# A mixture-of-experts stage on one core: the down product in three passes, combine weights through DMA and GpSimd

## The chip, the cores and the metric

The kernel runs on one core of a Trainium2 chip. The metric is the device time of one execution in microseconds. A core has five engines that run side by side and meet at semaphores: TensorE (PE; its weight loads are PEld), VectorE (DVE), ScalarE (ACT), GpSimd (POOL) and SyncE (SP), which here issues DMA transfers. TensorE has two clock levels, 1.2 and 2.4 GHz; the granted clock in the profile is the share of the higher one.

## The reference, cut to what matters

The network has four layers on 4608 tokens of 128 channels (8 images of 24 by 24). The change is in the second, a mixture of eight experts and one shared expert, all 64 wide:

```
x_flat = layernorm(t)                                  # (4608, 128)
shared = silu(x_flat @ shared_gate) * (x_flat @ shared_up) @ shared_down
probs  = softmax(x_flat @ router)                      # (4608, 8)
combine[n, e] = probs[n, e] if e is one of the two largest of row n else 0
gate = silu(x_flat @ W_gate[e]);  up = x_flat @ W_up[e]
y    = (gate * up) @ W_down[e]
t    = t + shared + sum over e of combine[:, e] * y[e]
```

Every token goes through all eight experts; the combine weight, mostly zero, is multiplied into the hidden row ahead of the down product.

## The kernel before, in words

The program is a chain of blocks; a block ends when all engines are through with their part of it. Three of them matter here.

*The router* (lines 615 to 702) normalises and transposes the tokens. It keeps them twice in SBUF with channels on the partitions: `xTH`, rounded to the F32R format that TensorE takes in one pass, and `xTL`, the rounded-off rest.

*The weights block* (lines 704 to 741) finds the top two for the second half of the tokens (the first half was done earlier), and transposes all combine weights, in nine lots of 512 tokens, from tokens on partitions to experts on partitions. ScalarE writes each lot's rounded values into `cT` (L723) and VectorE the rests (L715).

*The expert block* (lines 767 to 960) goes over 12 chunks of 384 tokens. A chunk has five units: four pairs of experts (`k` 0 to 3, 128 hidden rows: two experts of 64) and the shared expert (`k` 4). Unit `u` counts through all 60. For a pair TensorE makes

- the gate product in three passes, high by high, high by low, low by high (`product3`, L807, L808, L811), into PSUM bank `q = u % 2`,
- the combine weights spread over the 64 rows of each expert, a product of `cT` with a matrix of ones (`sel`, L826), into bank 4,
- the up product in three passes into bank `2 + q`,
- the down product (L838), in full precision, from the hidden rows `h4`; the five units of a chunk add up in bank 5 or 6.

ScalarE takes the SiLU of the gate bank (`s4`, L879). VectorE multiplies bank 4 by it (`t4`, L918), and that by the up bank (`h4`, L923, in SBUF). For the shared expert gate and up lie in the two halves of one bank and VectorE multiplies once (L927). When a chunk is done, ScalarE copies its bank (`y4`, L892), TensorE transposes it in three pieces into bank 7 (L849, `back`) and VectorE adds it to the residual `R` (L907).

The order on each engine is written out by hand: TensorE issues `feed(u + 1)` and then `down(u)`; ScalarE runs one unit ahead. The first and last two chunks are straight code, the ten between them a hardware loop (`Fori`) over two chunks.

In the last two chunks VectorE also does the next layer's first statistics, one step `ahead(a)` for each of the last ten units: for `a` 0 to 5 three `bn_stats` (L941), with seven small instructions of `norm_moments` after every third; for `a` 6 to 8 three normalisations (L948). Between them GpSimd takes a power (`norm_rstd`, L158), and `ahead(6)` waits for the first one (`rs5`). Otherwise GpSimd only clears buffers at the start of this block (L770, L781), and SP writes zeros into the DRAM tensor `slots`, seven transfers of 768 KB (L792, L796).

Of the kernel before, what the change touches and what calls it, by code (L numbers as in the profile page):

```python
# [25 lines left out]
F32 = mybir.dt.float32  # L26
# [56 lines left out]
def metaformer_kernel(nc, A, out):  # L83
    ctx = ExitStack()
    with ctx:
# [40 lines left out]
        slots = nc.dram_tensor("slots", [2 * SLOTS + N, C], F32, kind="Internal").ap()  # L126

# [50 lines left out]
        sel = sb("sel", [P, E2 // 2 * P], F32R)  # L178
# [217 lines left out]
        with nc.Block() as block:  # L396
# [163 lines left out]
        dve3b, ex3, spl3, cps3, cH3, cL3, cz3, sl3, wz3 = (  # L560
            sem(n) for n in "dve3b ex3 spl3 cps3 cH3 cL3 cz3 sl3 wz3".split())
        cT = lsb("cT", [P, N], F32R)
# [51 lines left out]

        with nc.Block() as block:
            @block.gpsimd
            def _(pool):
                nc.gpsimd.memset(wd[H2:P, NB2 - 1, :], 0.0).then_inc(wz3, 1)
                pool.wait_ge(wz3, 1)
                nc.gpsimd.memset(cT[:].bitcast(F32), 0.0).then_inc(cz3, 1)  # L620
# [43 lines left out]
            def _(act):  # L664
# [11 lines left out]
                nc.scalar.activation(sel[:], konst[:, K_SEL:K_SEL + E2 * H2], ACT.Copy)  # L676
# [27 lines left out]
        with nc.Block() as block:  # L704
            @block.vector
            def _(dve):
# [5 lines left out]
                for b in range(NT // TB):  # L712
                    dve.wait_ge(cH3, b + 1)
                    at = slice(b * TB * P, (b + 1) * TB * P)
                    nc.vector.tensor_tensor(cT[32:32 + E2, at], bank[b % 8][:E2, :], cT[0:E2, at].bitcast(F32),  # L715
                                            ALU.subtract).then_inc(cL3, 1)

            @block.scalar
            def _(act):
                def high_weights(first, end):  # L720
                    for b in range(first, end):
                        act.wait_ge(cps3, b + 1)
                        nc.scalar.activation(cT[0:E2, b * TB * P:(b + 1) * TB * P], bank[b % 8][:E2, :],  # L723
                                             ACT.Copy).then_inc(cH3, 1)

                act.wait_ge(cz3, 1)
                high_weights(0, EARLY)
                act.wait_ge(sl3, 2)
                nc.scalar.activation(ex8[1], d8[1], ACT.Exp).then_inc(ex3, 1)
                high_weights(EARLY, NT // TB)  # L730

            @block.tensor
            def _(pe):
                for b in range(NT // TB):
                    if b == EARLY:
                        pe.wait_ge(spl3, 2)
                    if b >= 8:
                        pe.wait_ge(cL3, b - 7)
# [5 lines left out]
        s4 = [lsb(f"s4_{q}", [P, CH]) for q in range(2)]  # L744
        t4 = [lsb(f"t4_{q}", [P, CH]) for q in range(2)]
        h4 = [lsb(f"h4_{q}", [P, CH]) for q in range(2)]
        y4 = [lsb(f"y4_{p}", [P, CH]) for p in range(2)]
        g_ps, u_ps, s_ok, h_ok, dn, yS, zt = (sems(n) for n in "g_ps u_ps s_ok h_ok dn yS zt".split())
        cb_ps, t_ok, R_ok = sem("cb_ps"), sem("t_ok"), sem("R_ok")
# [3 lines left out]
        TRIPS = N // CH // 2  # L753
        UB = 2 * NB2
        UPT = 2 * (NB2 - 1)
# [1271 lines left out]
```

## Time and profile before

| | |
|---|---|
| median of 3 runs | 450.92 us (449.1 to 452.47) |
| the profiled execution | 448.98 us |
| its span, first to last instruction | 446.8 us |
| granted TensorE clock, mean | 0.865 |
| TensorE busy | 373.4 us, 84% of the span |
| VectorE, ScalarE, GpSimd busy | 305.2, 154.1, 127.8 us |

Busy time is the time in which an engine has an instruction in work. The ends of matrix products are modelled in the profile and neighbouring products overlap, so the distance from the start of one to the start of the next is what a product costs. Lines of the timeline give start, duration, engine and source line; "x3" behind a line means that three alike were merged; "q" behind an engine's name is its queue, and the bracket at the end is the idle time ahead of the instruction and what ended it. Times are microseconds from the start of the span.

### The profile page before, as it was taken

How to read it: one execution, taken by the hardware profiler on the slowest of the kernel's cores; microseconds unless marked ns; L12 is line 12 of the kernel's file. 1: busy time of each engine (PE TensorE's matmuls, PEld its weight loads, DVE VectorE, ACT ScalarE, POOL GpSimd, SP SyncE). 2: the span in 40 equal slices, each digit the busy share in tenths (PEclk: the TensorE clock that was granted, in tenths of full speed). 3: DMA queues.
4: the chain of work that ended last, by engine and by line, in shares of the span. 5: the costliest groups of instructions: out<-in, count | busy, mean ns of one | idle time of the engine just before them, and what ended most of it. 6: DMA issues, size and time to landing. Idle time of an engine off the chain costs nothing. (4 is left out here: it accounts for less than half of the span.)

```text
span 446.8 us, 6657 instructions
## 1 busy us (share of the span) xinstructions
PE 373.4 (84%) x2125; PEld 315.9 (71%) x2125; DVE 305.2 (68%) x949; ACT 154.1 (34%) x324; POOL 127.8 (29%) x141
## 2 busy tenths in 40 slices
PE   5955949968999999998756999999789796699880
PEld 5955949947888887887445899999779762693330
DVE  5846884885555566569656576876574969259997
ACT  2221154434333333332214455475465530240000
POOL 5750143006500000002000366010116567005773
PEclk9999555558999999999856599999999976699996
DMA  8930510005700000000011011111001011772335
GB/s 182 278 119 12 164 43 1 1 0 203 292 1 0 0 1 0 0 0 0 2 28 43 10 35 35 34 35 35 1 1 55 13 41 48 256 264 82 95 99 147
DMA packets 22890, 29.66 MB, mean 66 GB/s; under 512 B 4104, under 2 KB 18249, under 8 KB 22606
## 3 DMA queue, kind: packets, MB, share of 16 engines
q1 hardware_dynamic: 18350, 22.47, 17.1%
q0 software_dynamic: 1728, 3.54, 2.6%
q10 hardware_dynamic: 2784, 3.29, 2.1%
q8 instruction: 15, 0.25, 0.2%
q14 instruction: 13, 0.11, 0.1%
HBM read 13.48 MB, written 12.78 MB: 59 GB/s over the span
## 5 line engine op out<-in xcount | busy, mean ns | idle before, releaser
L158 POOL TENSOR_TENSOR rstd<-sm,neg_half 128x9 f32<-128x9 f32 x10 | 18.0, 1804 | 203.3 <-DVE sm L152 203.3
L807 PE MATMUL ps<-wide,gu_w 128*128 (+1 forms) x108 | 51.9, 481 | 2.2 <-PEq L704 2.2
L879 ACT ACTIVATE s<-ps 128x384 f32<-128x384 f32 (+1 forms) x60 | 29.5, 492 | 67.4 <-PE ps L811 67.0
L1767 PE MATMUL ps<-V,wide 128*128 128x129 f32 x400 | 51.3, 276 | 0.0
L838 PE MATMUL ps<-h,wd 128*128 128x384 f32 x120 | 49.8, 497 | 1.6 <-DVE h L923 1.2
L1767 PEld LDWEIGHTS ps<-V,wide 128*128 128x128 f32 x400 | 48.4, 192 | 0.1
L918 DVE TENSOR_TENSOR t<-ps,s 128x384 f32<-128x384 f32 x48 | 26.8, 557 | 30.3 <-ACT s L879 30.0
L1811 PE MATMUL ps<-ew,xTd 128*128 128x512 f32 x72 | 38.2, 669 | 3.6 <-DVE R L1480 3.5
L1480 DVE SCALAR_TENSOR_TENSOR R<-ps,dense_w,R 128x128 f32<-128x128 f32 x144 | 38.3, 343 | 1.3 <-PE ps L1811 1.1
L1232 DVE TENSOR_REDUCE mx<-ps 128x1 f32<-128x576 f32 (+1 forms) x40 | 29.8, 749 | 12.8 <-PE ps L1735 12.7
L811 PE MATMUL ps<-wide,gu_w 128*128 (+1 forms) x108 | 37.0, 343 | 0.3 <-DVE t L918 0.3
L808 PE MATMUL ps<-wide,gu_w 128*128 (+1 forms) x108 | 37.0, 342 | 0.0
L1578 ACT ACTIVATE wide<-ps 128x576 f32<-128x576 f32 (+1 forms) x40 | 25.9, 649 | 30.1 <-PE ps L1747 30.0
L1142 POOL DMA_INDIRECT slots<-xn,sidx x27 | 26.4, 976 | 26.0 <-DVE sidx L1359 18.8
L923 DVE TENSOR_TENSOR h<-ps,t 128x384 f32<-128x384 f32 x48 | 26.8, 558 | 4.3 <-DVE t L918 3.1
L1735 PE MATMUL ps<-Q,K 97*128 97x288 f32 x80 | 22.5, 372 | 7.4 <-DVE mx L1232 4.6
L1811 PEld LDWEIGHTS ps<-ew,xTd 128*128 128x128 f32 x72 | 14.2, 212 | 19.9 <-issue 11.7
L1173 POOL DMA_INDIRECT xn<-slots,gidx x18 | 18.6, 1035 | 31.6 <-DMA slots<-wide 26.4
L807 PEld LDWEIGHTS ps<-wide,gu_w 128*128 128x128 f32 x108 | 20.8, 193 | 8.7 <-issue 2.4
L808 PEld LDWEIGHTS ps<-wide,gu_w 128*128 128x128 f32 x108 | 20.9, 194 | 6.2
L838 PEld LDWEIGHTS ps<-h,wd 128*128 128x128 f32 x120 | 21.0, 188 | 5.7 <-DVE h L923 4.6
L811 PEld LDWEIGHTS ps<-wide,gu_w 128*128 128x128 f32 x108 | 20.7, 191 | 0.7 <-DVE t L918 0.7
(252 smaller groups left out, 810.8 us busy)
## 6 DMA issues: line engine op xcount, KB each, us to landing
slots<-zrow SPq DMA_DIRECT2D x7, 768.0 KB, 7.7
xe<-slots SPq DMA_DIRECT2D x16, 192.0 KB, 4.0
slots<-wide ACTq DMA_DIRECT2D x16, 192.0 KB, 2.9
xall<-in_x SPq DMA_DIRECT2D x8, 288.0 KB, 6.1
out<-R SPq DMA_DIRECT2D x9, 192.0 KB, 2.1
Q<-sQK SPq DMA_DIRECT2D x8, 144.0 KB, 2.4
K<-sQK SPq DMA_DIRECT2D x8, 144.0 KB, 2.5
ew<-in_ew SPq DMA_DIRECT2D x1, 1024.0 KB, 5.4
```

Source lines behind the costliest of these rows:

```text
L807: nc.tensor.matmul(o, gu_w[0][:, w], xTH[:, at], start=True, stop=False)
L808: nc.tensor.matmul(o, gu_w[0][:, w], xTL[:, at], start=False, stop=False)
L811: return nc.tensor.matmul(o, gu_w[1][:, w], xTH[:, at], start=False, stop=True)
L838: nc.tensor.matmul(bank[5 + p][:, :CH], wd[:, k, :], h4[q][:], start=k == 0, stop=k == NB2 - 1).then_inc(dn[q], 1)
L879: nc.scalar.activation(s4[q][:r], bank[q][:r, :CH], ACT.Silu).then_inc(s_ok[q], 1)
L918: d.did(nc.vector.tensor_tensor(t4[q][:], bank[4][:, :CH], s4[q][:], ALU.mult))
L923: nc.vector.tensor_tensor(h4[q][:], bank[2 + q][:, :CH], t4[q][:], ALU.mult).then_inc(h_ok[q], 1)
L1142: nc.gpsimd.indirect_dma_start(slots, bass.IndirectOffsetOnAxis(sidx[g % 2][:, t:t + 1], 0), xn_buffer(g)[:, t, :], None).then_inc(sc6[g % ...
L1232: nc.vector.tensor_reduce(mx[n % 2][:m, k:k + 1], halves(psum[e_pair(n, k)], m), AX.XY, ALU.max).then_inc(mx_ok, 1)
L1480: nc.vector.scalar_tensor_tensor(at, of, weight, at, ALU.mult, ALU.add).then_inc(s9, 1)
L1767: last = nc.tensor.matmul(bank[6 + k // 3][:, k % 3 * (C + 1):(k % 3 + 1) * (C + 1)], PT[n % 2][:, jk, i0:i0 + P], V[n % 2][:, jk, :], sta ...
L1811: last = nc.tensor.matmul(bank[b], xTd[:, (t - DENSE0) * P:(t - DENSE0 + 1) * P], ew[:, 4 * quad:4 * quad + 4, :].rearrange("c e f -> c (e ...
```

## The change

The combine weights are no longer split or multiplied out on TensorE. ScalarE copies them as they are; SP stores them to a DRAM tensor `combine_w` in two parts and loads them back, spread over the 64 rows of each expert, one chunk at a time into two buffers `cB` (`spread`, two DMAs of 393 KB each). The first two chunks are spread in the weights block, later ones when GpSimd has done all multiplies of two chunks before. GpSimd multiplies `cB` by the SiLU (`t4`); VectorE multiplies the up bank by `t4` in place, so that the hidden product stays in PSUM (three up banks, 2 to 4, in turn; the shared unit's product stays in its gate bank). ScalarE copies it rounded into `hH`, VectorE subtracts that from it into `hL`, and the down product is made in three F32R passes from `hH`, `hL` and a split weight `wdH`, `wdL`. The down product runs three units behind the feed (`LAG`). The loop is written out. GpSimd's buffer clears come one by one behind the multiplies of chunks 2 to 8, its two powers after the last multiply; SP's zero fills go between the spreads.

```diff
-        sel = sb("sel", [P, E2 // 2 * P], F32R)
+        wdH, wdL = (sb(n, [P, NB2, C], F32R) for n in ("wdH", "wdL"))
+        cB = [pt_tiles[0][:, 0:E2 // 2, 0:CH], pt_tiles[1][:, 0:E2 // 2, P:P + CH]]
+        def spread(sp, c):
+            at = slice(CH * c, CH * (c + 1))
+            by_half = combine_w[:, at].rearrange("(k two) n -> two k n", two=2)
+            for half in range(2):
+                sp.dma_start(cB[c % 2][H2 * half:H2 * (half + 1)],
+                             by_half[half:half + 1].to_broadcast([H2, E2 // 2, CH])).then_inc(cin[c % 2], 16)
...
-                for b in range(NT // TB):
-                    dve.wait_ge(cH3, b + 1)
-                    at = slice(b * TB * P, (b + 1) * TB * P)
-                    nc.vector.tensor_tensor(cT[32:32 + E2, at], bank[b % 8][:E2, :], cT[0:E2, at].bitcast(F32),
-                                            ALU.subtract).then_inc(cL3, 1)
+            @block.sync
+            def _(sp):
+                for j, (first, end) in enumerate(((0, EARLY), (EARLY, NT // TB))):
+                    at = slice(first * TB * P, end * TB * P)
+                    sp.wait_ge(cH3, end)
+                    sp.dma_start(combine_w[:, at], cT[:, at]).then_inc(cs[j], 16)
+                    if j == 0:
+                        sp.wait_ge(cs[0], 16)
+                        for c in range(2):
+                            spread(sp, c)
+                sp.wait_ge(cs[1], 16)
...
+                act.wait_ge(wz3, 1)
+                nc.scalar.activation(wdH[:], wd[:], ACT.Copy).then_inc(wdh, 1)
                 high_weights(EARLY, NT // TB)
...
+        CHUNKS = N // CH
+        UNITS = CHUNKS * NB2
+        LAG = 3
+        def shared(u):
+            return u % NB2 == NB2 - 1
+        def pair(u):
+            return (NB2 - 1) * (u // NB2) + u % NB2
+        def pair_unit(v):
+            return v // (NB2 - 1) * NB2 + v % (NB2 - 1)
+        def held(u):
+            return bank[u % 2][0:H2, :CH] if shared(u) else bank[2 + pair(u) % 3][:, :CH]
...
             @block.gpsimd
-                for ap, value in firsts:
-                    z.did(nc.gpsimd.memset(ap.bitcast(F32), value))
-                    z.wait()
+                for u in range(UNITS):
+                    if shared(u):
+                        continue
+                    v, c = pair(u), u // NB2
+                    pool.wait_ge(cin[c % 2], 32 * (c // 2 + 1))
+                    pool.wait_ge(s_ok, u + 1)
+                    if v >= 2:
+                        pool.wait_ge(h_ok, pair_unit(v - 2) + 1)
+                    nc.gpsimd.tensor_tensor(t4[v % 2][:], cB[c % 2][:, u % NB2, :], s4[u % 2], ALU.mult).then_inc(t_ok, 1)
+                    if v == 8:
+                        nc.gpsimd.memset(zrow[:], 0.0).then_inc(z4, 1)
+                    elif v > 8 and v - 9 < len(firsts):
+                        ap, value = firsts[v - 9]
+                        pool.wait_ge(t_ok, v + 1)
+                        z.did(nc.gpsimd.memset(ap.bitcast(F32), value))
+                        z.wait()
+                z.wait()
                 for g in range(BEFORE):
                     pool.wait_ge(var5, g + 1)
                     norm_rstd(GT, g, P, rs5)
             @block.sync
+                for c in range(2, 4):
+                    sp.wait_ge(t_ok, (NB2 - 1) * (c - 1))
+                    spread(sp, c)
                 sp.wait_ge(z4, 1)
+                for c in range(4, CHUNKS):
+                    sp.wait_ge(t_ok, (NB2 - 1) * (c - 1))
+                    spread(sp, c)
+                    for k in range(4 * (c - 4), min(4 * (c - 3), SLOTS // (SR * 12))):
+                        sp.dma_start(slots[k * SR * 12:(k + 1) * SR * 12, :].rearrange("(p t) c -> p t c", t=12),
+                                     zrow[:SR]).then_inc(zf4, 16)
+                    if c - 8 in range(NT // 12):
...
             @block.tensor
+                def feed(u):
+                    c, k = divmod(u, NB2)
+                    tokens = slice(CH * c, CH * (c + 1))
+                    if u >= 2:
+                        pe.wait_ge(s_ok, u - 1)
+                        if shared(u - 2):
+                            pe.wait_ge(hl_ok, u - 1)
+                    product3(bank[u % 2][:, :CH], slice(2 * k * P, (2 * k + 1) * P), tokens).then_inc(g_ps, 1)
+                    if not shared(u):
+                        v = pair(u)
+                        if v >= 3:
+                            pe.wait_ge(hl_ok, pair_unit(v - 3) + 1)
+                        product3(bank[2 + v % 3][:, :CH], slice((2 * k + 1) * P, (2 * k + 2) * P), tokens).then_inc(u_ps, 1)
+                def down(u):
...
+                    pe.wait_ge(hh_ok, u + 1)
+                    nc.tensor.matmul(o, wdH[:, k, :], hH[q][:], start=k == 0, stop=False)
+                    nc.tensor.matmul(o, wdL[:, k, :], hH[q][:], start=False, stop=False)
+                    pe.wait_ge(hl_ok, u + 1)
+                    nc.tensor.matmul(o, wdH[:, k, :], hL[q][:], start=False, stop=k == NB2 - 1).then_inc(dn, 1)
...
+                for u in range(UNITS + LAG):
+                    if u < UNITS:
+                        feed(u)
+                    if u >= LAG:
+                        down(u - LAG)
+                    c, k = divmod(u - LAG - 1, NB2)
+                    if k == 0 and c >= 1:
+                        back(c - 1)
+                back(CHUNKS - 1)
             @block.scalar
+                silu(0)
+                for u in range(UNITS + LAG + 1):
+                    if u + 1 < UNITS:
+                        silu(u + 1)
+                    if u < UNITS:
+                        high(u)
+                    c, k = divmod(u - LAG + 1, NB2)
+                    if k == 0 and c >= 1:
+                        channels(c - 1)
             @block.vector
+                def hidden(u):
+                    if shared(u):
+                        dve.wait_ge(s_ok, u + 1)
+                        nc.vector.tensor_tensor(held(u), bank[u % 2][H2:P, :CH], s4[u % 2][:H2], ALU.mult).then_inc(h_ok, 1)
+                    else:
+                        dve.wait_ge(u_ps, pair(u) + 1)
+                        dve.wait_ge(t_ok, pair(u) + 1)
+                        nc.vector.tensor_tensor(held(u), held(u), t4[pair(u) % 2][:], ALU.mult).then_inc(h_ok, 1)
+                def low(u):
+                    dve.wait_ge(hh_ok, u + 1)
+                    r = rows(u)
+                    nc.vector.tensor_tensor(hL[u % 3][:r], held(u), hH[u % 3][:r].bitcast(F32), ALU.subtract).then_inc(hl_ok, 1)
...
+                for u in range(UNITS + LAG + 2):
+                    if u < UNITS:
+                        hidden(u)
+                    if 1 <= u <= UNITS:
+                        low(u - 1)
+                    c, k = divmod(u - LAG - 2, NB2)
+                    if k == 0 and c >= 1:
+                        residual(c - 1)
+                    if UNITS - 2 * NB2 <= u < UNITS:
+                        if u == UNITS - 2 * NB2:
+                            dve.wait_ge(R_ok, CHUNKS // 2)
+                        ahead(u - UNITS + 2 * NB2)
+                residual(CHUNKS - 1)
```

## Rows read from the trace of the kernel before

**Rows 1.** Windows: stretch, length, busy time by engine, granted clock, DMA share, GB/s.
```profile
122.30:131.50 9.20, 9.20 (x46) 7.55 (x44) 5.45 (x11) 2.95 (x6) 0.00 (x0) 1.00 0.00 1
```

**Rows 2.** Timeline of a pair unit inside the loop: start, duration, engine, line.
```profile
125.34 0.34 PE L811 MATMUL ps<-wide,gu_w 128*128 x1
...
125.71 0.49 ACT L879 ACTIVATE s<-ps 128x384 f32<-128x384 f32 x1
...
126.05 0.34 PE L811 MATMUL ps<-wide,gu_w 128*128 x1
...
126.22 0.81 PE L838 MATMUL ps<-h,wd 128*128 128x384 f32 x2
...
127.92 0.34 PE L811 MATMUL ps<-wide,gu_w 128*128 x1
```

**Rows 3.** Timeline of the weights block and the start of the expert block.
```profile
96.27 0.59 ACT L723 ACTIVATE cT<-ps 8x512 fp32r<-8x512 f32 x1 [0.27 <-PE ps L740]
...
98.23 5.46 DVE L715 TENSOR_TENSOR cT<-ps,cT 8x512 fp32r<-8x512 f32 x9
...
101.02 1.63 ACT L723 ACTIVATE cT<-ps 8x512 fp32r<-8x512 f32 x3 [0.27 <-PE ps L740]
...
104.17 0.41 PE L807 MATMUL ps<-wide,gu_w 128*128 128x384 f32 x1 [2.18 <-PEq L704]
...
113.67 0.63 PE L807 MATMUL ps<-wide,gu_w 128*128 128x384 f32 x1
```

**Rows 4.** Timeline where chunk 11 begins and TensorE waits for VectorE.
```profile
205.97 0.56 DVE L923 TENSOR_TENSOR h<-ps,t 128x384 f32<-128x384 f32 x1
206.45 0.67 DVE L941 BATCH_NORM_STATS2 st<-R 128x6 f32<-128x128 f32 x3
...
206.58 0.91 PE L838 MATMUL ps<-h,wd 128*128 128x384 f32 x2 [0.96 <-DVE h L923]
...
207.04 0.64 PE L807 MATMUL ps<-wide,gu_w 128*128 128x384 f32 x1
...
207.51 0.33 PE L808 MATMUL ps<-wide,gu_w 128*128 128x384 f32 x1
```

**Rows 5.** Timeline of the end of the expert block.
```profile
212.37 0.85 DVE L948 TENSOR_SCALAR xn<-R,sm,rstd 128x128 f32<-128x128 f32 x3
...
217.98 0.91 PE L838 MATMUL ps<-h,wd 128*128 128x384 f32 x2 [0.45 <-DVE h L927]
...
220.06 0.56 DVE L907 TENSOR_TENSOR R<-R,ps 128x384 f32<-128x384 f32 x1 [2.13 <-PE ps L849]
```

**Rows 6.** Groups by line, GpSimd: count, busy us, mean ns of one, idle before.
```profile
L158 POOL TENSOR_TENSOR rstd<-sm,neg_half 128x9 f32<-128x9 f32 x10 | 18.0, 1804 | 203.3 <-DVE sm L152 203.3
...
L253 POOL TENSOR_TENSOR kvq<-scaled,bkvq 96x288 f32<-96x288 f32 x8 | 6.2, 791 | 2.6 <-DVE scaled L296 2.6
...
L781 POOL MEMSET Q<- 1x640 f32 x6 | 3.8, 627 | 0.3
...
L487 POOL TENSOR_TENSOR nmr<-sm,rstd 128x9 f32<-128x9 f32 x2 | 0.4, 208 | 0.2
```

**Rows 7.** DMA issues on the page: count, KB each, median us to landing.
```profile
K<-sQK SPq DMA_DIRECT2D x8, 144.0 KB, 2.5
```

**Rows 8.** Windows, in the midst of the zero fills; the last number is GB/s.
```profile
107.00:108.00 1.00, 1.00 (x5) 1.00 (x4) 0.13 (x2) 0.49 (x1) 0.93 (x2) 0.53 1.05 424
```

**Rows 9.** Timelines of GpSimd and VectorE in the first block.
```profile
13.99 1.54 POOL L253 TENSOR_TENSOR kvq<-scaled,bkvq 96x288 f32<-96x288 f32 x2
...
15.04 0.53 DVE L280 TENSOR_TENSOR sm<-st 96x12 f32<-96x12 f32 x1
15.49 0.17 DVE L281 TENSOR_TENSOR sm<-st 96x12 f32<-96x12 f32 x1
```

**Rows 10.** Windows in the stage behind: busy time by engine, then the granted clock.
```profile
225.00:230.00 5.00, 1.31 (x5) 0.59 (x4) 2.17 (x6) 1.23 (x2) 0.00 (x0) 0.50 0.26 59
315.00:320.00 5.00, 2.75 (x22) 2.31 (x21) 2.20 (x10) 3.01 (x8) 2.00 (x2) 1.00 0.00 0
```

More of the change, by code:

```diff
@@ L741, in _ @@
                     last.then_inc(cps3, 1)
-        s4 = [lsb(f"s4_{q}", [P, CH]) for q in range(2)]
+        s4 = [wstage[:, q * CH:(q + 1) * CH] for q in range(2)]
         t4 = [lsb(f"t4_{q}", [P, CH]) for q in range(2)]
[L746 to L749, printed above, removed]
+        hH = [lsb(f"hH{q}", [P, CH], F32R) for q in range(3)]
+        hL = [lsb(f"hL{q}", [P, CH], F32R) for q in range(3)]
+        y4 = [xTf[p][:] for p in range(2)]
+        g_ps, u_ps, s_ok, t_ok, h_ok, hh_ok, hl_ok, dn, yS, zt, R_ok, wdl = (
+            sem(n) for n in "g_ps u_ps s_ok t_ok h_ok hh_ok hl_ok dn yS zt R_ok wdl".split())
         zrow = lsb("zrow", [P, 12, C])
@@ L852, in trip @@
-                def trip(i, first, final):
-                    for u in range(UB):
-                        if u + 1 < UB:
-                            feed(i, u + 1)
-                        elif not final:
-                            feed(i + 1, 0)
-                        down(i, u)
-                        if u == 1 and not first:
-                            back(i - 1, 1)
-                        if u == NB2 + 1:
-                            back(i, 0)
-                pe.wait_ge(wz3, 1)
@@ new lines, in back @@
+                def back(c):
+                    pe.wait_ge(yS, c + 1)
+                    if c:
+                        pe.wait_ge(R_ok, c)
+                    for t in range(3):
+                        last = nc.tensor.transpose(bank[7][:, t * P:(t + 1) * P], y4[c % 2][:, t * P:(t + 1) * P], ident)
+                    last.then_inc(zt, 1)
+                pe.wait_ge(wz3, 1)
+                for u in range(UNITS + LAG):
[6 more added lines that the diff above has]
+                        back(c - 1)
@@ L894, in _, with silu @@
-                silu(0, 0)
-                trip(0, False)
-                with act.Fori(1, TRIPS - 1) as i:
-                    trip(i, False)
-                trip(TRIPS - 1, True)
+                def silu(u):
+                    act.wait_ge(g_ps, u + 1)
+                    if u >= 2:
+                        if shared(u - 2):
+                            act.wait_ge(h_ok, u - 1)
+                        else:
+                            act.wait_ge(t_ok, pair(u - 2) + 1)
+                    r = rows(u)
+                    nc.scalar.activation(s4[u % 2][:r], bank[u % 2][:r, :CH], ACT.Silu).then_inc(s_ok, 1)
@@ new lines, in high, with channels @@
+                def high(u):
+                    act.wait_ge(h_ok, u + 1)
+                    if u >= 3:
+                        act.wait_ge(dn, u - 2)
+                    nc.scalar.activation(hH[u % 3][:rows(u)], held(u), ACT.Copy).then_inc(hh_ok, 1)
+                def channels(c):
+                    act.wait_ge(dn, NB2 * (c + 1))
+                    if c >= 2:
+                        act.wait_ge(zt, c - 1)
+                    nc.scalar.activation(y4[c % 2], bank[5 + c % 2][:, :CH], ACT.Copy).then_inc(yS, 1)
```

147 lines of the change are left out of this document (27 added, 120 removed).

## The prediction

> **What bounds the kernel now.** I read the busy time of each engine in one stretch of the stage first, then the order of time inside one unit, then the two ends of the stage, and last the rows that price the new work. In the stretch from 122.3 to 131.5 us, about one chunk of 384 tokens, TensorE is busy all of 9.20 us at full clock, VectorE 5.45, ScalarE 2.95 and GpSimd nothing [rows 1]. So TensorE sets the pace and three engines have room. Inside a unit the single passes (F32R) follow each other every 0.175 us: the last pass of a gate product starts at 125.34 and that of the up product at 126.05, four passes later. The last pass of the next up product starts at 127.92, so a pair unit takes 1.87 us [rows 2]. It holds seven such passes, 1.225 us; what is left, 0.645 us, is the full-precision down product. The chunks agree: chunk 1 begins at 113.67 and chunk 11 at 207.04, ten chunks of 9.34 us [rows 3, 4]. The stage runs from 104.17 to 220.06 + 0.56 = 220.62 us [rows 3, 5].
>
> **What is removed from TensorE.** Each of 48 pair units loses the selection product (0.175), and each of 60 down products goes from 0.645 to three passes, 0.525. A pair unit becomes 9 × 0.175 = 1.575 us. The shared unit becomes 6 × 0.175 = 1.05, and with it come the three transposes of the output, 0.34. A chunk would be 4 × 1.575 + 1.05 + 0.34 = 7.69 us, 1.65 under now, if TensorE could still run without waiting. That is the whole of the possible gain, some 18 us.
>
> **The path that is put in its place.** The hidden products now stay in PSUM, and a bank is free only when the low half has been taken from it. For pairs there are three banks; for gate products two, and the shared unit's product lies in its gate bank. So the gate product of the second pair after a shared unit s, unit s + 2, waits for low(s). VectorE's order is hidden(u), then low(u − 1): low(s) stands behind hidden(s + 1), and that waits for ScalarE and GpSimd on unit s + 1. Counted from the start of gate(s + 1): its last pass starts at 0.35; ScalarE starts 0.37 later and takes 0.49 [rows 2], 1.21. GpSimd's multiply is not in the trace at 384 columns. The nearest rows are 0.791 for 288 columns and 0.208 for 9, so 0.99 for 384 [rows 6]. Releases between engines cost 0.03 to 0.08; I take 0.05, so hidden(s + 1) starts at 2.30. Two VectorE instructions without a wait between them start 0.48 apart and take 0.56, and TensorE starts 0.05 after VectorE's end [rows 4]: 2.30 + 0.48 + 0.56 + 0.05 = 3.39. A restart costs 0.11 more (0.93 from L838 to the L808 that follows in [rows 4], against 0.645 + 0.175 where it runs on). So gate(s + 2) starts 3.50 us after gate(s + 1), where TensorE has work for 1.575. TensorE stands still for 1.9 us in each chunk, and a chunk is 3.50 + 3 × 1.575 + 1.05 + 0.34 = 9.61 us, not 7.69. Against 9.34 that is 0.27 more. Queued behind this wait on TensorE are all later feeds and the down products of the last two units.
>
> In the other units the same loop has room: up(u + 3) waits for low(u), which ends at 1.575 + 3.39 = 4.97, and TensorE gets there at 3 × 1.575 + 0.525 = 5.25. ScalarE's second copy (another 0.49) and the second VectorE pass stay below 1.575 a unit.
>
> The in-place write of hidden into PSUM has no row. Between 0 more and one more pass over 384 columns (0.4 us, from 0.48 a pass) I take 0, since every VectorE row here with one PSUM operand costs the same 0.56; the 0.4 would be paid in each chunk, 4 to 5 us.
>
> **Ends of the stage, and what moves.** *Start.* Before, the block with the weights ends with VectorE's low halves at 98.23 + 5.46 = 103.69 and the first product comes at 104.17 [rows 3]. These halves go; SP takes their place. The first store of weights can go at 96.86, the second after the last ScalarE copy at 102.65. A store of 144 KB took 2.5 us to landing [rows 7], which gives 105.15. But between them SP queues two spreads of 0.79 MB, 3.7 us at the 424 GB/s of [rows 8], which begin about 100.3 and end near 104. The block ends between 104.7 and 106.7; I take 105.5, so +1.8. *Chunk 0* took 9.50; it loses four selections and four down products and has only two of the new ones, since these run three units behind: −0.70 − 2.58 + 1.05 = −2.2, of which the wait for the first low half gives back about 0.6: −1.6. *Ten chunks*: 10 × 0.27 = +2.7. *Memsets*: 27 of them, the common one 0.63 [rows 6], now stand between the multiplies. GpSimd's 0.99 + 0.63 + two waits exceeds 1.575, so it slips up to 0.4 within a chunk and catches up while TensorE waits; +0.3 over three chunks. *Spreads*: a chunk's DMA may start when the multiplies of two chunks before are done, some 11 us ahead, and 0.79 MB take 2 us; even behind four zero fills of 0.77 MB it lands in 13 of some 21. Nothing, unless the queue holds it 8 us longer. The last zero fill is issued over two chunks before the end: 0. The wdH copy and the wdL difference lie under waits: 0. Loop unrolling: its price now is inside the 1.87; 0.
>
> *End.* This is the largest term. The last two chunks carry the next stage's statistics on VectorE, and ahead(6), in unit 56, waits for the first power on GpSimd. Before, GpSimd was idle there. Now both powers (1.80 each [rows 6]) stand behind the last multiply, that of unit 58. From the first gate product of chunk 11: VectorE comes about 1.3 late, as the seven moments instructions (0.17 each [rows 9]) find no room in chunk 10; hidden(55) starts at 2.30 + 1.3 = 3.6, gate(56) at 3.6 + 0.48 + 0.56 + 0.05 + 0.11 = 4.8, gate(58) two units later at 7.95, its multiply ends 1.26 + 0.99 later at 10.2, and the power at 12.05. Only then do three ahead steps (0.77 each, from three in 0.85 [rows 5]) and four passes of 0.48 run to hidden(59) at 16.3; then 0.56, copy 0.49, low 0.56 and three releases: 18.05. Before, the last down product took 0.91 and the end came 2.64 after its start [rows 5]; with a last pass of 0.34 it is 2.07: 20.1. Before it was 220.62 − 207.04 = 13.6. So +6.5.
>
> Sum: 1.8 − 1.6 + 2.7 + 0.3 + 6.5 = +9.7 us. The profiled execution took 448.98 us (span 446.8 and 2.2 around it), 1.9 under the median of the runs and just under the lowest. 448.98 + 9.7 = 458.7; from the median it is 460.6. I forecast 460.
>
> **GpSimd and VectorE at once.** One row shows them in each other's way: a VectorE sum of two SBUF operands took 0.53 where the next takes 0.17, and it ended with the GpSimd operation that ran from 13.99 to 15.53 [rows 9]. Hidden and low read one operand each from PSUM, and no row shows such an instruction beside a multiply. The Trainium skill ("SBUF — State Buffer", Who interferes with whom) says that only two SBUF inputs or a two-port mode collide with GpSimd's reads. By that rule only the moments suffer, up to 1 us at the end, and the sum stays; the trace agrees as far as it goes. Without it, low would wait out each multiply: the third rival.
>
> **The rivals.** *Faster: TensorE keeps its pace.* Had low(s) its turn before hidden(s + 1), the loop would close with 7.69 a chunk: 10 × 1.92 less than forecast, 441 us. For it: TensorE is the bound now and loses 18 us of work. Against it: the written order, and no idle engine can reorder it. Faster than before begins where the 3.50 falls under 3.2, and by over 1% near 2.2, before the multiply could end. 7%. *Same:* multiply 0.8 (the 288-column price), shorter releases and a part of the end hidden: −0.35 × 11 − 3 = 453 us. 18%. *Slower still:* PSUM write at 0.4 more, or VectorE held off by each multiply, 0.8 a pair unit in three of a chunk: 2.4 × 11 = 26, to 486; the PSUM write alone 465. 12% together. *Clock:* full clock held in a stretch with TensorE busy 2.75 of 5 us; it stood at half with 1.31 of 5 busy [rows 10]. The new stage has 7.69 of 9.61 us. If half were granted, a chunk's products would take 15.4: 60 us more, 520. 3%. The Trainium skill ("TensorE: Matmul & The Clock Gate", HAM oscillation — how this bites in real kernels) warns that waits between bursts of matmuls bring the slow clock back; the first row of the two bears it out, the second shows a share of work well under this stage's at full clock.
>
> **How the numbers follow.** Forecast 60%: 460. Its own bounds: multiply 0.8 to 1.2 gives −2 to +5; the start −0.8 to +1.2; the PSUM write up to +5. With the case of no change the range is 452 to 470; beyond lie 7 + 8 + 3 in 100. What a measurement of this kernel can tell from no change is about 1%, 446.4 to 455.4 us: faster 0.07, same 0.20, slower 0.73.
>
> **What would show it.** In the changed profile: one TensorE gap of near 1.9 us in each chunk, ended by VectorE's low subtraction; chunks 9.6 apart; multiplies of 0.99; first product near 106; VectorE idle for about 4 us in the last chunk until GpSimd's power. A chunk spacing under 9 would break the first step, a multiply far from 1.0 its size, an end under 16 us after chunk 11's start the last.

## The result and the profile after

The changed kernel takes 474.06 us (median of 472.82 to 475.29) against 450.52 for the kernel before: a ratio of 1.049, 95% interval 1.0445 to 1.0541. That is slower by 23.5 us, above the range of the prediction (452 to 470). The profiled execution has a span of 473.5 us, 26.7 more than before; the two profiled executions (448.98 and 475.29 us) stand 2.8 us further apart than the medians. The tables by stage go by these two.

The stage by chunk: chunk 0 starts with the first pass of a gate product (L850) at 109.66, chunk 1 at 117.92, chunk 11 at 219.27, and the last residual sum (L954) ends at 243.43. The chunks from 0 to 10 take 8.26, 9.71, 10.19, 10.16, 10.16, 10.08, 9.95, 11.41, 10.04, 9.87 and 9.78 us; before, the mean of chunks 1 to 10 was 9.34 [rows 3, 4]. So:

| part of the span | before | after | difference | forecast |
|---|---|---|---|---|
| up to the first product | 104.17 | 109.66 | +5.5 | +1.8 |
| chunk 0 | 9.50 | 8.26 | -1.2 | -1.6 |
| chunks 1 to 10 | 93.37 | 101.35 | +8.0 | +3.0 (2.7 + 0.3) |
| chunk 11 to the end of the stage | 13.58 | 24.16 | +10.6 | +6.5 |
| all stages behind | 226.18 | 230.07 | +3.9 | 0 |
| sum | 446.8 | 473.5 | +26.7 | +9.7 |

The windows of the ten chunks in the middle (length, busy time by engine, granted clock, DMA share, GB/s) answer to [rows 1]:

```profile
117.92:219.27 101.35, 81.52 (x452) 76.60 (x451) 57.72 (x121) 50.11 (x111) 53.44 (x68) 0.98 0.47 133
```

TensorE, which before stood still in these ten chunks only for the 0.96 us of [rows 4], now does so for 19.8 of 101.35 us, 2.0 a chunk. The timeline of chunk 10 shows where. It starts with gate(s + 1) and ends with gate(s + 2):

```profile
209.49 0.42 PE L850 MATMUL ps<-wide,gu_w 128*128 128x384 f32 x1
...
210.15 0.57 DVE L940 TENSOR_TENSOR ps<-ps,wstage 64x384 f32<-64x384 f32 x1
...
210.30 0.49 ACT L911 ACTIVATE wstage<-ps 128x384 f32<-128x384 f32 x1
...
210.75 0.48 ACT L917 ACTIVATE hH<-ps 64x384 fp32r<-64x384 f32 x1
...
210.92 1.00 POOL L814 TENSOR_TENSOR t<-wide,wstage 128x384 f32<-128x384 f32 x1 [1.93 <-ACT wstage L911]
...
212.02 0.57 DVE L944 TENSOR_TENSOR ps<-ps,t 128x384 f32<-128x384 f32 x1 [0.72 <-POOL t L814]
212.50 0.54 DVE L949 TENSOR_TENSOR hL<-ps,hH 64x384 fp32r<-64x384 f32 x1
...
213.18 0.42 PE L850 MATMUL ps<-wide,gu_w 128*128 128x384 f32 x1 [1.87 <-DVE hL L949]
```

Hidden(s), the product of the shared unit, is there at 210.72 and its high half at 211.23, but low(s) waits until 212.50 behind hidden(s + 1), which waits for the multiply. TensorE's wait of 1.87 ends with low(s), the row with 64 partitions.

The start, in the timeline of the block of the weights, and the spreads in the view of the DMA issues:

```profile
99.11 2.49 ACT L740 ACTIVATE cT<-ps 8x512 f32<-8x512 f32 x5 [1.21 <-PE ps L758]
99.52 2.64 SPq L624 DMA_DIRECT2D wide<-combine_w  x4
102.20 0.50 SPq L728 DMA_DIRECT2D combine_w<-cT  x1
...
109.66 0.66 PE L850 MATMUL ps<-wide,gu_w 128*128 128x384 f32 x1 [8.84 <-PEq L713]
```
```profile
DMA packets 1104, 1.66 MB, mean 162 GB/s; under 512 B 72, under 2 KB 1096, under 8 KB 1096
...
wide<-combine_w SPq DMA_DIRECT2D x4, 384.0 KB, 6.2
```

All arithmetic of the block is over at 101.60. SyncE issues the second store at 102.20, behind four spreads of 384 KB, and the block waits for it until 109.6. In the second fence, from 99.5 to 109.7 us, 1.66 MB move at a mean of 162 GB/s; the traffic fills 29 of that view's 40 slices, which gives some 220 GB/s while it lasts (estimate: 162 × 40 / 29), not the 424 of [rows 8]. TensorE idles for 8.84 us and starts chunk 0 at half clock (passes 0.32 apart).

The end, in the timeline from chunk 11 on:

```profile
219.27 0.42 PE L850 MATMUL ps<-wide,gu_w 128*128 128x384 f32 x1
...
224.31 0.66 PE L850 MATMUL ps<-wide,gu_w 128*128 128x384 f32 x1 [2.91 <-DVE hL L949]
...
230.04 0.34 PE L850 MATMUL ps<-wide,gu_w 128*128 128x384 f32 x1
...
231.39 1.01 POOL L814 TENSOR_TENSOR t<-wide,wstage 128x384 f32<-128x384 f32 x1 [0.94 <-issue]
```
```profile
232.36 3.56 POOL L159 TENSOR_TENSOR rstd<-sm,neg_half 128x9 f32<-128x9 f32 x2
234.20 0.86 DVE L969 TENSOR_SCALAR xn<-R,sm,rstd 128x128 f32<-128x128 f32 x3 [5.81 <-POOL rstd L159]
...
242.87 0.56 DVE L954 TENSOR_TENSOR R<-R,ps 128x384 f32<-128x384 f32 x1 [2.25 <-PE ps L887]
```

VectorE waits 5.81 us for the power behind the last multiply. The clock in the windows (the third number from the end; 1.00 is 2.4 GHz, 0.50 is 1.2):

```profile
182.00:184.00 2.00, 2.00 (x7) 2.00 (x8) 0.26 (x1) 0.82 (x2) 0.10 (x1) 0.51 1.07 329
222.00:224.00 2.00, 0.00 (x0) 0.00 (x0) 1.97 (x7) 0.48 (x1) 0.48 (x1) 0.75 0.01 4
224.00:230.00 6.00, 5.70 (x18) 5.73 (x19) 3.17 (x14) 1.74 (x4) 1.56 (x2) 0.51 0.00 0
264.00:274.00 10.00, 7.66 (x33) 6.96 (x33) 5.28 (x14) 3.76 (x6) 0.00 (x0) 0.50 0.13 30
```

Half clock was granted for 3.4 us in chunk 7 (11.41 us where its neighbours take 9.95 and 10.04), and again from 223.0, within the wait that ends at 224.31, until 229.8. The last row lies 20.6 to 30.6 us behind the stage's end; the same stretch of the kernel before had 0.67, for about 3 us of full clock in it:

```profile
241.00:251.00 10.00, 7.43 (x36) 6.68 (x36) 5.52 (x15) 3.94 (x7) 0.00 (x0) 0.67 0.13 30
...
331.80 0.69 DVE L1232 TENSOR_REDUCE mx<-ps 64x1 f32<-64x576 f32 x1
```

The last of these VectorE maxima, 111.18 us behind the stage's end before, comes 114.21 behind it after (357.64 - 243.43): 3.0 of the 3.9 us are lost by there, in the same 702 matrix products.

```profile
357.64 0.69 DVE L1261 TENSOR_REDUCE mx<-ps 64x1 f32<-64x576 f32 x1
```

### The profile page after: what moved, and what is told of

It is laid out like the page before. It is cut to its first block and busy times, and to the rows that moved or that the text cites. A ratio compares the mean times of both kernels' runs of the same rounds, so it can differ in the third digit from the quotient of the medians.

```text
span 473.5 us, 6654 instructions
## 1 busy us (share of the span) xinstructions
PE 366.4 (77%) x2137; PEld 323.5 (68%) x2137; DVE 302.6 (64%) x953; ACT 178.5 (38%) x384; POOL 171.0 (36%) x188
## 5 line engine op out<-in xcount | busy, mean ns | idle before, releaser
L814 POOL TENSOR_TENSOR t<-wide,wstage 128x384 f32<-128x384 f32 x48 | 48.4, 1009 | 101.5 <-ACT wstage L911 89.9
L850 PE MATMUL ps<-wide,gu_w 128*128 128x384 f32 x108 | 41.0, 379 | 31.9 <-DVE hL L949 22.9
L944 DVE TENSOR_TENSOR ps<-ps,t 128x384 f32<-128x384 f32 x48 | 27.2, 566 | 48.3 <-POOL t L814 45.8
L1796 PE MATMUL ps<-V,wide 128*128 128x129 f32 x400 | 53.3, 283 | 0.0
L1796 PEld LDWEIGHTS ps<-V,wide 128*128 128x128 f32 x400 | 50.3, 198 | 0.1
L911 ACT ACTIVATE wstage<-ps 128x384 f32<-128x384 f32 (+1 forms) x60 | 29.3, 489 | 48.0 <-PE ps L852 47.5
L850 PEld LDWEIGHTS ps<-wide,gu_w 128*128 128x128 f32 x108 | 21.8, 202 | 36.6 <-issue 34.9
L851 PE MATMUL ps<-wide,gu_w 128*128 128x384 f32 x108 | 38.5, 356 | 0.0
L852 PE MATMUL ps<-wide,gu_w 128*128 128x384 f32 x108 | 38.3, 354 | 0.0
L917 ACT ACTIVATE hH<-ps 128x384 fp32r<-128x384 f32 (+1 forms) x60 | 29.4, 489 | 21.2 <-DVE ps L944 18.4
L949 DVE TENSOR_TENSOR hL<-ps,hH 128x384 fp32r<-128x384 f32 (+1 forms) x60 | 32.8, 548 | 0.4
L879 PE MATMUL ps<-hL,wdH 128*128 128x384 f32 x60 | 21.6, 360 | 4.1 <-DVE hL L949 4.0
L851 PEld LDWEIGHTS ps<-wide,gu_w 128*128 128x128 f32 x108 | 22.0, 204 | 0.0
```

The lines of the kernel that those rows point to most:

```text
L814: nc.gpsimd.tensor_tensor(t4[v % 2][:], cB[c % 2][:, u % NB2, :], s4[u % 2], ALU.mult).then_inc(t_ok, 1)
L850: nc.tensor.matmul(o, gu_w[0][:, w], xTH[:, at], start=True, stop=False)
L851: nc.tensor.matmul(o, gu_w[0][:, w], xTL[:, at], start=False, stop=False)
L852: return nc.tensor.matmul(o, gu_w[1][:, w], xTH[:, at], start=False, stop=True)
L949: nc.vector.tensor_tensor(hL[u % 3][:r], held(u), hH[u % 3][:r].bitcast(F32), ALU.subtract).then_inc(hl_ok, 1)
L1796: last = nc.tensor.matmul(bank[6 + k // 3][:, k % 3 * (C + 1):(k % 3 + 1) * (C + 1)], PT[n % 2][:, jk, i0:i0 + P], V[n % 2][:, jk, :], sta ...
```

## The experiments

Theory A is that of the prediction with these corrections: separate waits, each with its place (start, low(s), memsets, powers), which add up. The rivals stand in each expectation. All edits are to the changed kernel, and are shown cut to the lines that matter. From each trace, one execution a kernel: first product, mean of chunks 1 to 10, chunk 11 to the end of the stage, and the rest of the span.

| run | median us | against before (95%) | first product | chunk | last chunk | rest |
|---|---|---|---|---|---|---|
| kernel before | 450.52 | | 104.17 | 9.34 | 13.58 | 226.2 |
| changed kernel | 474.06 | 1.049 (1.045 to 1.054) | 109.66 | 10.14 | 24.16 | 230.1 |
| e1_wait | 469.68 | 1.041 (1.034 to 1.049) | 103.17 | 10.14 | 24.15 | 230.8 |
| e2_low | 461.11 | 1.019 (1.012 to 1.026) | 109.51 | 8.78 | 22.51 | 232.4 |
| e3_pow | 469.67 | 1.040 (1.034 to 1.047) | 109.54 | 10.27 | 18.55 | 227.6 |
| e4_half | 461.89 | 1.022 (1.014 to 1.030) | 109.18 | 9.43 | 20.80 | 229.1 |
| e5_all | 448.61 | 0.992 (0.989 to 0.996) | 103.23 | 8.78 | 17.88 | 231.4 |
| e6_hold | 439.06 | 0.971 (0.965 to 0.977) | 103.15 | 7.92 | 17.82 | 229.9 |
| e7_early | 437.04 | 0.966 (0.960 to 0.972) | 103.00 | 8.20 | 12.22 | 228.7 |
| e8_memset | 475.08 | 1.049 (1.042 to 1.056) | 109.41 | 10.24 | 24.30 | 230.7 |
| e9_spread | 432.76 | 0.956 (0.951 to 0.961) | 103.86 | 7.79 | 12.48 | 230.5 |
| e10_hold | 449.09 | 0.995 (0.991 to 0.999) | 109.57 | 7.96 | 21.65 | 228.1 |
| e11_f32 | 435.83 | 0.963 (0.956 to 0.970) | 103.48 | 8.27 | 12.15 | 226.3 |

**The second store (e1_wait).**

```diff
             # SyncE, block of the weights
-            sp.wait_ge(cs[1], 16)
             # SyncE, expert block
             for c in range(4, CHUNKS):
                 sp.wait_ge(t_ok, (NB2 - 1) * (c - 1))
+                if c == 5:
+                    sp.wait_ge(cs[1], 16)
```

> The wait of SyncE for the second store of weights is moved from the end of the weights block to just ahead of the first spread that reads what it wrote (that of chunk 5). Theory A (the block with the weights ends late because that store, issued at 102.20, lies on its queue behind four spreads that move 1.57 MB until about 109.5): the first product comes when the last ScalarE copy and the transposes are done, near 102.5 instead of 109.66, but the first multiply still needs chunk 0's spread, about 104.5; the stage begins 6 to 7 us earlier and the whole kernel is 5 to 7 us faster, 467 to 469. Rival B (the spreads themselves hold chunk 0: the multiply waits for the same bytes wherever the wait stands): first product early, but chunk 0 longer by the same 5 to 7 us; no change, 472 to 475.

The timeline has the store at 102.09, behind the spreads as before, and the first product 1.1 us later:

```profile
102.09 0.49 SPq L728 DMA_DIRECT2D combine_w<-cT  x1
...
103.17 0.41 PE L850 MATMUL ps<-wide,gu_w 128*128 128x384 f32 x1 [2.46 <-PEq L713]
```

The first product comes 6.5 us earlier, and chunk 0 takes 8.03: theory A. The span of the trace falls by 5.9 us (the stage ends 6.7 earlier, the rest is 0.7 longer), the median by only 4.4 (expected 5 to 7).

**The low half first (e2_low).**

```diff
+                first = u >= 1 and shared(u - 1)
+                if first:
+                    low(u - 1)
                 if u < UNITS:
                     hidden(u)
-                if 1 <= u <= UNITS:
+                if 1 <= u <= UNITS and not first:
                     low(u - 1)
```

> VectorE takes the low half of a shared unit ahead of the next hidden product. Theory A (TensorE stands still once a chunk because low(s) waits behind hidden(s+1), which waits for ScalarE and GpSimd on unit s+1): low(s) starts when ScalarE's copy of hidden(s) is done, about 1.3 us earlier; the gap of 1.9 to 2.1 us goes below 0.9 and chunks come every 8.7 to 9.0 us instead of 10.1; ten chunks 11 to 14 us, the kernel 460 to 463. Rival B (GpSimd's multiply with its waits and memsets is the pace whatever the order, 4 multiplies and one gap a chunk): the gap moves to another product, chunks stay at 9.8 to 10.2, 471 to 475.

```profile
189.76 1.07 DVE L949 TENSOR_TENSOR hL<-ps,hH 128x384 fp32r<-128x384 f32 x2
...
189.94 0.99 POOL L814 TENSOR_TENSOR t<-wide,wstage 128x384 f32<-128x384 f32 x1 [1.50 <-DVE ps L940]
190.98 0.42 PE L850 MATMUL ps<-wide,gu_w 128*128 128x384 f32 x1 [0.76 <-DVE hL L949]
191.03 0.57 DVE L944 TENSOR_TENSOR ps<-ps,t 128x384 f32<-128x384 f32 x1 [0.20 <-POOL t L814]
```

In the timeline low(s) now runs ahead of hidden(s + 1), in one row with low(s - 1); gate(s + 2) starts while the multiply is just ending, and hidden(s + 1) comes after it. The gap is 0.76 instead of 1.87, the chunk 8.78, and the kernel 13 us faster than the changed one. So the order on VectorE held TensorE, not the pace of GpSimd.

**The first power earlier (e3_pow).**

```diff
                 # GpSimd, behind each multiply
+                if u == UNITS - 7:
+                    pool.wait_ge(var5, 1)
+                    norm_rstd(GT, 0, P, rs5)
...
-            for g in range(BEFORE):
-                pool.wait_ge(var5, g + 1)
-                norm_rstd(GT, g, P, rs5)
+            pool.wait_ge(var5, 2)
+            norm_rstd(GT, 1, P, rs5)
```

> GpSimd takes the first power after the multiply of unit 53 instead of after that of unit 58; the second stays last. Theory A (VectorE's 5.8 us of idle time at 228.4 to 234.2 are the wait for a power that is queued behind the last multiply, and the half clock behind it follows from TensorE's idle time): the 5.8 us go, chunk 11 to the end of the stage takes 16.5 to 19 us instead of 24.2, the kernel 466 to 469. Rival B (the end is paced by the half clock that was granted before the power was due, from 222 to 230): 1 to 3 us, 471 to 473.

The last chunk falls by 5.6 us, from 24.16 to 18.55: the wait of 5.8 was the one for the power. TensorE still idles 2.9 us ahead of gate(56), for low(54) behind the statistics, and gate(56) to gate(58) takes 4.77 us, from 226.8 on at half clock, so rival B has the other part. In this trace chunks 3 and 10 took 11.49 and 11.34, and the median gained 4.4 of the 5 to 8 expected.

**Half a multiply (e4_half).** This kernel leaves out half of each multiply: the other half of `t4` stays zero, so it is a probe and no version to use.

```diff
-nc.gpsimd.tensor_tensor(t4[v % 2][:], cB[c % 2][:, u % NB2, :], s4[u % 2], ALU.mult)
+nc.gpsimd.tensor_tensor(t4[v % 2][:, :CH // 2], cB[c % 2][:, u % NB2, :CH // 2], s4[u % 2][:, :CH // 2], ALU.mult)
```

> Leaves work out: GpSimd multiplies only the first 192 of 384 columns (the other half of its result stays zero), all waits kept. By the slope between 1.01 us at 384 columns and 0.79 at 288 the multiply takes 0.56. Theory A (the multiply lies on the chain from gate(s+1) to gate(s+2), once a chunk): the gap shrinks by 0.45, the chunks with memsets also lose their excess of 0.3; chunks 9.3 to 9.6 instead of 10.1, the kernel 5 to 8 us faster, 466 to 469. Rival B (GpSimd paces every unit): four times 0.45 a chunk, chunks near 8.5, 455 to 458. Rival C (TensorE or VectorE paces): no change.

The multiply takes 0.59, the chunks 9.28 to 9.47: 0.71 less each on average. The chunks without memsets (1, 9 and 10) fall by 0.42, the multiply once a chunk; the rest is memsets that now fit and the spell at half clock in chunk 7, which is gone. Rival B, four times the multiply, would have been 8.5. The kernel gained 12 us, more than expected: chunk 11 and chunk 0 pay for the multiply too (3.4 and 0.4), and none of the ten chunks ran at half clock.

**The three together (e5_all)**: the diffs of e1, e2 and e3.

> The three edits together: the wait for the second store moved to the spread of chunk 5, the low half of a shared unit taken ahead of the next hidden product, the first power after the multiply of unit 53. Theory A (three separate losses, which add): stage from 103.2, chunks 8.8, chunk 11 to the end 17 to 18.5; -6.5 in the start, -13.5 in ten chunks, -6 at the end, of which the next stage gives some back: 449 to 453, as the kernel before. Rival B (the losses overlap, since the clock of TensorE falls wherever it waits): 455 to 460.

They add, to within 4 us: 448.61 is 25.5 under the changed kernel, where the three alone took 4.4, 13.0 and 4.4 off the median. Chunk 0 gives back 1.2 of the start (9.42 us): with the store out of the way, the first multiply waits until 105.80 for its spread, and TensorE stands still for 1.82 us behind it. The kernel is within 1% of the one before the change, though its chunks have 1.65 us less of TensorE's work.

**A bank for the shared product (e6_hold, e10_hold).** The first has the three edits as well, the second nothing else.

```diff
-return bank[u % 2][0:H2, :CH] if shared(u) else ...     # held(u)
+return bank[6][0:H2, :CH] if shared(u) else ...
-pe.wait_ge(hl_ok, u - 1)                                # feed, behind a shared unit
+pe.wait_ge(h_ok, u - 1)
-o, q = bank[5 + c % 2][:, :CH], u % 3                   # down; channels likewise
+o, q = bank[5][:, :CH], u % 3
                     # ScalarE: channels(c - 1) moved ahead of silu(u + 1)
```

> As the three together, and besides the shared unit's product gets a bank of its own (the second bank of the down product, which keeps one; ScalarE then copies a chunk's output ahead of the next silu), so that gate(s+2) waits for hidden(s) alone and no longer for low(s). Theory A (the rest of the gap, 0.9 us a chunk and 1.2 with memsets, is the held gate bank): chunks 7.8 to 8.1, 7 to 9 us less than with the three edits, 441 to 445, faster than the kernel before. Rival B (GpSimd's multiply of 1.0 and its waits and memsets leave no more than 8.7 a chunk): within 2 us of the three edits. Rival C (one bank for the down product makes TensorE wait for ScalarE's copy once a chunk, 0.5 to 1.4 us): 445 to 450.

> The changed kernel with one edit: the shared unit's product has a bank of its own, and the down product one bank. Theory A (the one gap of TensorE a chunk is the held gate bank, nothing else): chunks without memsets 7.7, those with memsets 8.2 to 8.4; 10 chunks 20 us less, start and end as in the changed kernel; 453 to 456, about the kernel before. Rival B (without the low half taken first the wait only moves, to the up product three pairs on, which waits for low(u)): chunks 8.5 to 9, 460 to 464.

With this one edit the chunks with neither memsets nor statistics (1 and 9) take 7.59 and 7.66, the whole of the work that the prediction counted (chunk 10, with statistics, 8.03), and the kernel takes 449.09, within 1% of the kernel before; expected were 453 to 456, but chunk 11 and the rest gained 2.5 and 2.0 as well. In the timeline of e10_hold gate(s + 2) follows gate(s + 1) by 1.65 us while the multiply runs:

```profile
125.43 0.42 PE L850 MATMUL ps<-wide,gu_w 128*128 128x384 f32 x1
...
126.86 1.02 POOL L814 TENSOR_TENSOR t<-wide,wstage 128x384 f32<-128x384 f32 x1 [1.94 <-ACT wstage L911]
...
127.08 0.34 PE L850 MATMUL ps<-wide,gu_w 128*128 128x384 f32 x1
```

So the held gate bank alone was the gap. With the other three edits it gives 439.06.

**Memsets and statistics (e8_memset, e7_early, e9_spread).** The memsets go into the block ahead of the stage, all at once; in e7 also `UNITS - 2 * NB2` becomes `UNITS - 4 * NB2` for the statistics, and the powers follow the multiplies of units 43 and 48. In e9 the statistics are cut up:

```diff
-                if u % 3 == 2:
-                    norm_moments(f, ins, GT, g, P, EPS_C, var5)
+    # stats_of(g): three bn_stats, then the moments in four pieces, "yield" behind each;
+    # next_stage(): both groups, then the nine normalizations one by one
+                if UNITS - 5 * NB2 + 1 <= u < UNITS:
+                    next(ahead, None)
```

> The changed kernel with nothing but the 27 memsets moved into the block ahead of the stage. Theory A (each of the seven chunks with memsets pays 0.3, since GpSimd's multiply, memset and two waits take 1.78 where a unit has 1.575): chunks 2 to 8 fall from 10.1 to 9.8, 2.0 to 2.5 us in all, 471 to 472. Rival B (memsets collide with VectorE where they go): the product of that block later by 1 to 4 us, first product later, 473 to 476.

> As the one before, and besides the 27 memsets moved into the block ahead of the expert stage, where GpSimd has nothing to do, and the statistics of the next stage with both powers two chunks earlier. Theory A (memsets cost 0.3 in each of seven chunks, the statistics and the 2.3 us of normalization lie on VectorE's path in the last chunk): 2 us for the memsets and 3 to 5 at the end, 435 to 440. Rival B (VectorE's sums of two SBUF operands in the block of the weights collide with the memsets): that block grows by 1 to 4 us and eats it up; 440 to 444.

> As the version with early statistics, but these are cut into 23 pieces, one a unit over the last 24 units, and the second power comes a chunk later. Theory A (in that version the ninth and tenth chunk took 11.25 and 8.62 instead of 7.67, because seven statistics instructions at a time stand ahead of a hidden product, one of them held 1.00 us beside a multiply, and because the multiply of the next chunk waited for a power that waited for them): these chunks fall to 7.7 to 8.2, 3 to 4.5 us less, 433 to 434. Rival B (the power itself, 1.80 us, does not fit beside four multiplies in a chunk): 1.5 us of it stay, 435 to 437.

By its time e8 shows nothing (475.08), and rival B is not the reason: the first product comes at 109.41, not later. By its chunks it shows two things that cancel: seven chunks take 9.76 to 9.78, with nothing left of the 0.3 that chunks with memsets paid, and three take 11.33 to 11.35. In each of those three the clock fell for a spell:

```profile
124.00:126.00 2.00, 2.00 (x9) 2.00 (x8) 1.02 (x2) 0.54 (x2) 0.21 (x1) 0.65 0.00 0
155.00:157.00 2.00, 2.00 (x10) 2.00 (x9) 1.02 (x2) 0.62 (x2) 0.21 (x2) 0.72 0.09 17
186.00:188.00 2.00, 2.00 (x11) 2.00 (x10) 1.02 (x2) 0.75 (x2) 0.34 (x2) 0.79 0.21 86
```

A spell at half clock costs 1.57 us (11.34 against 9.77). In e7 the last chunk takes 12.22 instead of 17.82, but the statistics then weigh on their own chunks. Its timeline has one row like that of [rows 9]:

```profile
179.65 1.00 DVE L143 TENSOR_TENSOR sm<-st 128x9 f32<-128x9 f32 x1
180.58 0.16 DVE L144 TENSOR_TENSOR sm<-st 128x9 f32<-128x9 f32 x1
```

The first sum of two SBUF operands ran from 179.65 to 180.65, as long as GpSimd's multiply (179.62 to 180.63), the next 0.16. Hidden and low, with one operand in PSUM, keep 0.57 and 0.55 beside a multiply (low in 32 of 48 pair units of e7). The normalisations, 0.34 each alone, are held as well: in e11 six of nine take 0.71 to 1.16. In pieces (e9) chunks 9 and 10 fall from 11.25 and 8.62 to 8.35 and 7.67, and the kernel is the fastest: 432.76, 4.4% under the kernel before.

**One full-precision down product (e11_f32).** As e9, with the hidden product in SBUF, no high and low halves, and

```diff
-nc.tensor.matmul(o, wdH[:, k, :], hH[q][:], start=k == 0, stop=False)
-nc.tensor.matmul(o, wdL[:, k, :], hH[q][:], start=False, stop=False)
-nc.tensor.matmul(o, wdH[:, k, :], hL[q][:], start=False, stop=k == NB2 - 1).then_inc(dn, 1)
+nc.tensor.matmul(o, wd[:, k, :], h4[q][:], start=k == 0, stop=k == NB2 - 1).then_inc(dn, 1)
```

> The down product of the version with cut statistics put back to one full-precision pass with one hidden copy; the combine weights still spread by DMA and multiplied on GpSimd. Theory A (TensorE paces that version, so the split of the down product is worth its passes): a pair unit 6 x 0.175 + 0.645 = 1.695, the shared one 0.525 + 0.645 and 0.34 of transposes, a chunk 8.29 against 7.67: 7 us slower than with split halves, 439 to 442. Rival B (ScalarE and VectorE, with 20 fewer instructions in a chunk and a copy less on every chain, win back what TensorE loses): within 2 us of it.

The ten chunks, here and then in e9:

```profile
111.13:193.87 82.74, 82.74 (x403) 68.80 (x401) 42.22 (x96) 29.76 (x61) 42.92 (x43) 1.00 0.59 162
```
```profile
111.33:189.20 77.87, 77.53 (x451) 75.76 (x451) 64.20 (x145) 51.51 (x111) 42.87 (x42) 1.00 0.62 173
```

TensorE paces both, with 8.27 a chunk (8.29 worked out), and the split halves win 4.9 us in this stretch. In the time of the whole kernel less than the 7 expected is left of it: the medians differ by 3.1 us and their intervals overlap, and the two profiled spans are the same (432.4 and 432.1), since the rest was 4.0 longer in the trace of e9. So most of what e9 gains on the kernel before is there without the split, 10.6 us of it in the ten chunks (82.74 against 93.37 in the kernel before); and the split brings VectorE and ScalarE 44 us more work in them (the busy times of the two rows).

## Why the prediction was wrong

The direction and the main step were right; the size was not (+23.5 against +9.7). Between the two profiles 17.0 us were missed: 3.7 in the start, 0.4 in chunk 0, 5.0 in the ten chunks (1.8 the chain from gate to gate, 1.7 memsets, 1.4 clock), 4.1 at the end and 3.9 behind the stage.

**Right.** The step "low(s) stands behind hidden(s + 1)" is in the trace as written, and e2 and e10 show it by taking it away. TensorE's chunk of 7.69 us is real: 7.6 to 7.7 in e10. The gap was sized 1.9 and is 1.86 to 1.96 in the chunks without memsets; the chain from gate to gate was 3.50 and is 3.61 to 3.79 there: in the rows above ScalarE starts 0.81 behind the gate (0.72) and GpSimd 0.13 behind ScalarE's end (0.05). The multiply took 1.01 (0.99), and the write into PSUM in place 0.57 (0 more). Chunks without memsets or half clock take 9.79 on average (9.61): 1.8 of the 5.0 us that I missed in the ten chunks. GpSimd beside VectorE cost nothing in the changed kernel: no moment fell beside a multiply, and low took 0.55 in both cases, so the rival in which low waits out each multiply is out. The row of 1.00 in e7 agrees with what the Trainium skill ("SBUF — State Buffer", Who interferes with whom) says of two SBUF operands. Two numbers of the prediction do not follow from its own: with 9.7 us to make up in 11 chunks, faster than before begins where the 3.50 falls under 2.6, not 3.2; and the memsets were summed over three chunks, where 27 of them stand in seven.

**The start, +5.5 for +1.8.** The step that failed is "two spreads, 3.7 us at the 424 GB/s of the zero fills". They moved at some 220 GB/s, and the block, which waits for the store behind them, ended when they were through. I had the queue right and the rate wrong: a rate taken from transfers of another shape. What of the shape halves it was not tried. e1 shows the place: 6.5 us.

**The memsets, +2.0 for +0.3.** The step "it slips up to 0.4 within a chunk and catches up while TensorE waits" failed: memset chunks took 10.08 against 9.79 (chunk 7 without its spell at half clock), in each of seven chunks. e8 shows 9.77 in the same chunks without them. About half of the difference from e8 lies in the units behind the gap, about half in the chain of the gap (up to 3.92 from gate to gate, 3.69 in e8). Chunk 3, from its first gate product:

```profile
137.82 0.42 PE L850 MATMUL ps<-wide,gu_w 128*128 128x384 f32 x1
...
138.38 0.49 ACT L917 ACTIVATE hH<-ps 128x384 fp32r<-128x384 f32 x1 [0.55 <-DVE ps L944]
138.76 0.49 ACT L911 ACTIVATE wstage<-ps 128x384 f32<-128x384 f32 x1
...
139.48 0.99 POOL L814 TENSOR_TENSOR t<-wide,wstage 128x384 f32<-128x384 f32 x1 [1.11 <-DVE ps L940]
```

GpSimd has caught up, since it idles for 1.11 us ahead of its multiply. But the SiLU that it waits for stands on ScalarE behind the copy of hidden(s - 1), and that had waited for a slipped multiply; so the SiLU starts 0.94 behind its gate, not 0.81 as in e8, and the multiply 1.66 and not 1.43 (0.1 of this is there in chunk 9 too, which has no memset).

**The end, +10.6 for +6.5.** Of its steps gate(56) came 5.04 behind gate(55) (4.8), gate(58) 5.73 later (3.15), and the end 13.39 behind that (12.15). The queue of multiply and power is right, as e3 shows with 5.6 us. The middle term failed: it was worked out at full clock, and TensorE came out of a wait of 2.9 us, which was forecast as 3.2, at half of it, with 0.32 a pass for 0.175 (2.6 us over 18 passes).

**The clock.** I held it for a rival of all or nothing, 3 in 100. It came in pieces: 1.4 us in chunk 7, 2.6 in the middle term of the end, and 3.0 of the 3.9 behind the stage, for which the sum had no term at all. The ten inner chunks of the changed kernel, e1, e3 and e8, with a gap of 1.86 to 2.11 us a chunk, had 1, 1, 2 and 3 spells; those of e2, e4, e5, e6, e9, e10 and e11, with no gap over 1.57, ran at 1.00, as did those of e7, with a single one of 1.97. Which chunk is hit, these runs don't tell. The Trainium skill ("TensorE: Matmul & The Clock Gate", A second HAM failure mode: psum-queue depth-cycling) describes a kernel whose short idle times between groups of matmuls, at PSUM banks in turn, make the clock swing. The four traces with the long gap agree, with 1.57 us a spell in e8; why seven to nine of their ten chunks were spared is open.

**Open.** The rest of the span was 226.2 us in the kernel before and 226.3 to 232.4 in the others, whose code behind the stage is the same. Up to the last of the VectorE maxima above, it goes with the clock: in the kernel before, e4, e10 and e11 half clock was granted for 30.6 to 30.7 us of that stretch, and it took 110.8 to 111.2; in the changed kernel, e1, e5, e6 and e8 for 41.0 to 41.2, and it took 114.2 to 114.3, with the other four traces between or, in e2, above (43.1 and 115.3). What decides when the clock rises there was not tried, nor what makes up the rest of the 3.9 us.

## What to carry to other kernels

A gain on the engine that sets the pace is only had when each buffer that it fills comes free in time: list, for each bank, the last reader, and what stands ahead of that reader on its own engine. Here one held bank turned 18 us of saved work into a loss, and one bank taken from the down product gave 14 of them back in the ten chunks (79.6 against 93.4 in the kernel before). Price a transfer by a row of its own shape, ask of each wait that is moved what else stands behind it, and when a wait of two microseconds enters a loop of matmuls, price some spells at half clock too.

## What the runs showed of the hardware

A spread of a chunk's weights by DMA (384 KB, rows of 384 values repeated over 64 partitions) took 6.2 us to landing (median) with four in flight, some 220 GB/s in the changed kernel, against 424 for the zero fills of the kernel before. TensorE's clock fell to half in 1 to 3 of ten chunks with a wait of 1.86 to 2.11 us each (changed kernel, e1, e3, e8), at 1.57 us a spell, and not in others that look alike. A VectorE sum of two SBUF operands, 0.17 us alone, was held for 1.00 by a multiply on GpSimd (e7); instructions with one operand in PSUM kept their 0.55 to 0.57. A VectorE multiply that writes its own PSUM bank in place took 0.57, as one that writes SBUF does (0.56).
